# A delta-rule attention, mixture and decay attention kernel: the delta loop's instruction queues rearranged, decay tables stored inside the loop, and the decay attention's key scaling moved to GpSimd

## The chip, the core and the metric

The kernel runs on 1 core of one Trainium2 chip. The metric is the device time of one execution in microseconds (us); the median of several executions is given. All data is fp32.

## The reference

The input `x` has 4 batches of 1024 tokens with 128 channels. Four blocks are added to it, each of the layer-normed `x`:

```
x = x + delta_attention(layernorm(x))     # 8 heads of 128, 3 key/value pairs per token
x = x + mixture(layernorm(x))             # 15 experts of 128, softmax router, best 3, one shared expert
x = x + decay_attention(layernorm(x))     # 2 heads of 64
x = x + mixture(layernorm(x))
```

The delta attention, for each head, token by token (q, k and v come from a projection, a causal convolution of 4 taps and a silu; k and q are normed; `gt` is a decay, `bt` a step size):

```
S = S * exp(gt)
for i in range(3):
    S = S + bt_i * outer(k_i, v_i - k_i @ S)
o = q @ S;  out = (rmsnorm(o) * rms_weight * silu(gate)) @ Wo
```

The decay attention, for each head, token by token: `state = (1 - w)[:, None] * state + outer(k, v); out = r @ state`, where `w` and `r` are sigmoids of projections.

## The kernel before

The program has five stages, each a block of five instruction queues (TensorE `pe`, ScalarE `act`, VectorE `dve`, GpSimd `pool`, and `sp`, which issues DMAs) that wait for each other through semaphores. Each queue runs strictly in the order in which it is written.

**Prologue** (`prologue`). It norms `x` into `g.xn`, and makes the decays. For each of the 8 heads TensorE multiplies (line 213), ScalarE takes the exponential into `g.ex` (line 255) and VectorE masks the result (line 355, 128x1024 elements). The masked table of a head is stored to memory as four DMAs of 128 KB (`keep_table`, line 129): three from SP, one from ScalarE. The loop reads these tables back (`dec_load`, lines 541 and 542), each head's when its first step comes.

**Delta attention** (`delta_attention`). The work of a head is cut into 16 steps of 64 tokens of all 4 batches (two chunks of 32 tokens each, `cc` 0 and 1), so there are 128 steps. A software pipeline runs over `f`. In one frame every engine does one piece of three steps: the newest step `f` (keys and query: `k_tile`, `tap0` to `tap3`, `ktr`, `ksum_`, `es_`, `kr`, `gram`, `ap`), a step `c = f - 11` (values and the inverse of a triangular matrix: `v_tile`, `vtr`, `vr`, `zm`, `zev`, `wm`, `w12`, `m3`, `yev`), and the step `r = c - 1` before it, which goes through the recurrence. The recurrence of one step is, for `cc` 0 and then 1: `ks` (TensorE, line 1068), `rhs_` (VectorE, 901), `w_` (TensorE, 1078), `wev` (ScalarE, 762, writes `ws`), `sr` (TensorE, 1088), and `sup` (VectorE, 912, writes the new state `S`, with `Sg` from GpSimd's `sg`, 675). The outputs `o_` (TensorE, 1103 and 1104) go through `mo_` (ScalarE, 820), `fo_` (GpSimd, 684 and 686), `osb_` (828), `ot` (1221), `og_` (1001), `out` (1228) and `acc_` (1009).

GpSimd's `subst` (707 and 710) does the substitution inside triangular blocks of 32 rows for groups of four steps; once per group, so in every fourth frame, ScalarE copies a finished group transposed (`xt`, line 862, 96x1024) and SP stores it.

`m3` (line 1213) is eight small matrix products of 96 rows, with 64 columns of `Zt` as weights and 32 moving columns, and of its result only 32 rows are used (`yev` and the copies before it). The order of a frame is a list of calls per engine at the end of each block, written by hand or by a search; nothing else sets it.

**Mixture** (`normed_mixture`), twice, which the change does not touch.

**Decay attention** (`decay_attention`). Eight tiles of 512 tokens are projected (`tile`), into the tiles `rF`, `kB`, `F` and `V`. Then, for each batch, levels 0 to 7 double the length of the blocks whose tokens may see each other. A level below `MASKED` = 7 is a near step: TensorE multiplies 64-wide squares (`near`, line 1757), VectorE merges them under a mask into `Pc` (1945 for level 0, `COPY_PREDICATED` at 1948 for the others), and VectorE then scales `kB`, `rF` and `F` for the next level (`merge`, lines 1962, 1963 and 1965, 128x512 elements each). Level 7 is a far step: TensorE multiplies just the new corner (1770), ScalarE copies it straight into `P` (1861), VectorE only scales. `spread` (1869, ScalarE) copies `Pc` into `P` once a batch's last near step is done. Levels 0 and 1 of batches 0 to 2 are put between the tiles, everything else behind them. At the end TensorE turns `kB` (1791) and the outputs are made.

## Time and profile before

| | us |
|---|---|
| median of 3 runs (3137.80 to 3139.36) | 3138.93 |
| the profiled execution, its own time | 3139.86 |
| its span in the trace | 3138.0 |
| TensorE busy (93% of the span) | 2919.0 |
| VectorE busy (79%) | 2486.9 |
| ScalarE busy (75%) | 2346.9 |
| GpSimd busy (63%) | 1977.9 |

The profiled execution is one of its own, 0.9 us slower than the median. Its span begins with the first instruction on the core. The prologue takes it from 0 to 72.5 us, the delta loop to 2417, the first mixture to 2680, the decay attention to about 2860 and the second mixture to the end. "Busy" is the time in which an engine has at least one instruction running, so a queue that has no gap in the trace can still be slowed by the gaps that its own pipeline leaves.

### The profile page before, as it was taken

How to read it: one execution, taken by the hardware profiler on the slowest of the kernel's cores; microseconds unless marked ns; L12 is line 12 of the kernel's file. 1: busy time of each engine (PE TensorE's matmuls, PEld its weight loads, DVE VectorE, ACT ScalarE, POOL GpSimd, SP SyncE). 2: the span in 40 equal slices, each digit the busy share in tenths (PEclk: the TensorE clock that was granted, in tenths of full speed). 3: DMA queues.
4: the chain of work that ended last, by engine and by line, in shares of the span. 5: the costliest groups of instructions: out<-in, count | busy, mean ns of one | idle time of the engine just before them, and what ended most of it. 6: DMA issues, size and time to landing. Idle time of an engine off the chain costs nothing. (4 is left out here: it accounts for less than half of the span.)

```text
span 3138.0 us, 84065 instructions
## 1 busy us (share of the span) xinstructions
PE 2919.0 (93%) x27212; PEld 2241.5 (71%) x27212; DVE 2486.9 (79%) x5731; ACT 2346.9 (75%) x7723; POOL 1977.9 (63%) x3127
## 2 busy tenths in 40 slices
PE   5569999999999999999999999999987999768999
PEld 3448888888888888888888888888776444455444
DVE  5669999999999999999999999999754455594544
ACT  4769999999999999999999999999754443314443
POOL 1588888888888888888888888888831000100000
PEclk8779999999999999999999999999998999868999
DMA  5457777777777777777777777777532323002242
GB/s 108 123 147 179 190 187 180 180 184 174 184 187 191 182 182 182 178 179 182 193 184 182 183 179 182 180 189 181 154 96 75 152 102 152 10 3 78 107 160 115
DMA packets 588208, 482.91 MB, mean 154 GB/s; under 512 B 464784, under 2 KB 504368, under 8 KB 581632
## 3 DMA queue, kind: packets, MB, share of 16 engines
q1 hardware_dynamic: 579328, 474.39, 57.4%
q8 instruction: 223, 3.65, 0.5%
q10 hardware_dynamic: 8448, 3.15, 0.4%
q14 instruction: 209, 1.71, 0.2%
HBM read 285.53 MB, written 191.86 MB: 152 GB/s over the span
## 5 line engine op out<-in xcount | busy, mean ns | idle before, releaser
L953 DVE SCALAR_TENSOR_TENSOR conv_k<-PP,tk,conv_k 128x256 f32<-128x256 f32 x1536 | 718.5, 479 | 101.0 <-ACT conv_k L772 75.7
L953 DVE SCALAR_TENSOR_TENSOR conv_v<-PP,tv,conv_v 128x256 f32<-128x256 f32 x1152 | 540.5, 478 | 57.4 <-ACT conv_v L772 43.1
L710 POOL TENSOR_TENSOR X<-X,tmp 96x31 f32<-96x31 f32 (+15 forms) x992 | 534.3, 539 | 77.8
L707 POOL TENSOR_TENSOR tmp<-At,X 96x31 f32<-96x31 f32 (+15 forms) x992 | 486.7, 491 | 63.3 <-DMA At<-n_d 5.1
L1114 PE MATMUL PP<-xn,wk 128*128 128x268 f32 x1024 | 342.5, 418 | 41.4 <-DVE conv_k L953 29.7
L675 POOL TENSOR_TENSOR Sg<-S,gend 128x512 f32<-128x512 f32 x256 | 266.6, 1041 | 63.3 <-DVE S L912 63.3
L744 ACT ACTIVATE recA<-TG,es 96x128 f32<-96x128 f32 x1024 | 285.0, 367 | 6.3 <-DVE es L946 6.3
L693 POOL TENSOR_TENSOR rk<-ss,half 96x8 f32<-96x8 f32 x128 | 209.0, 1633 | 125.9 <-DVE ss L921 119.6
L1078 PE MATMUL RB<-rhs,Yf 96*96 96x128 f32 x2048 | 269.7, 274 | 18.7 <-DVE rhs L901 18.4
L772 ACT ACTIVATE conv_k<-PP,tk 128x256 f32<-128x256 f32 x512 | 245.2, 480 | 46.6 <-PE PP L1114 26.1
L1068 PE MATMUL RA<-S,kqgB 128*96 128x128 f32 x2048 | 276.1, 278 | 1.0 <-DVE S L912 1.0
L736 ACT ACTIVATE recA<-TG 128x128 f32<-128x128 f32 x1024 | 267.0, 309 | 9.8 <-PE TG L1165 9.6
L1088 PE MATMUL RA<-ws,recB 96*128 96x128 f32 x2048 | 273.8, 277 | 0.2 <-ACT ws L762 0.2
L1078 PEld LDWEIGHTS RB<-rhs,Yf 96*96 96x96 f32 x2048 | 241.9, 163 | 42.9 <-DVE rhs L901 30.3
L1088 PEld LDWEIGHTS RA<-ws,recB 96*128 96x128 f32 x2048 | 262.2, 194 | 8.0 <-ACT ws L762 0.6
L1177 PE MATMUL TG<-kq 128*96 128x128 f32 x1888 | 254.2, 277 | 1.7 <-ACT recA L744 1.5
L736 ACT ACTIVATION_READ_ACCUMULATOR recA<-TG 128x1 f32 x1024 | 245.8, 243 | 0.0
L1068 PEld LDWEIGHTS RA<-S,kqgB 128*96 128x96 f32 x2048 | 233.6, 163 | 12.9 <-DVE S L912 4.1
L1177 PEld LDWEIGHTS TG<-kq 128*96 128x96 f32 x1888 | 215.6, 163 | 19.7 <-ACT recA L744 7.9
L660 POOL TENSOR_TENSOR kqgA<-kq,gdec 128x768 f32<-128x768 f32 x128 | 203.5, 1590 | 34.0 <-ACT kq L813 26.0
L1114 PE MATMUL PP<-xn,wv 128*128 128x268 f32 x768 | 220.1, 394 | 1.2 <-DVE conv_k L953 1.2
L1114 PEld LDWEIGHTS PP<-xn,wk 128*128 128x128 f32 x1024 | 162.5, 198 | 72.3 <-issue 32.0
(292 smaller groups left out, 6578.4 us busy)
## 6 DMA issues: line engine op xcount, KB each, us to landing
kqg_d<-kqgA SPq DMA_DIRECT2D x128, 512.0 KB, 6.4
kqgB<-kqg_d SPq DMA_DIRECT2D x128, 512.0 KB, 4.4
rec_d<-recA SPq DMA_DIRECT2D x128, 480.0 KB, 3.4
recB<-rec_d SPq DMA_DIRECT2D x128, 480.0 KB, 6.1
f1gates<-f1gates_d SPq DMA_DIRECT2D x24, 1024.0 KB, 6.8
f2gates<-f2gates_d SPq DMA_DIRECT2D x24, 1024.0 KB, 6.9
gdec<-gdec_d SPq DMA_DIRECT2D x128, 128.0 KB, 5.8
apk_d<-apkA SPq DMA_DIRECT2D x128, 128.0 KB, 3.3
```

Source lines behind the costliest of these rows:

```text
L675: nc.gpsimd.tensor_tensor(Sg[:, :, :], S[cc][:, :, :], d.broadcast_to([128, B, 128]), ALU.mult).then_inc(sg_ev[cc], 1)
L707: nc.gpsimd.tensor_tensor(t, At[q % 2][:, j, j + 1:].unsqueeze(2).broadcast_to(sh), X[q % 2][:, j, 0:cols].unsqueeze(1).broadcast_to(sh), ...
L710: nc.gpsimd.tensor_tensor(x, x, t, ALU.subtract).then_inc(sub_ev, 1)
L736: last = nc.scalar.activation(recA[N % 2][:, u * 128:(u + 1) * 128], TG[:, u, :], ACT.Square, accum_out=ksum[:, u:u + 1])
L744: last = nc.scalar.activation(recA[N % 2][0:R, u * 128:(u + 1) * 128], TG[0:R, u, :], ACT.Copy, scale=es[:, u, TC - 1:TC])
L772: nc.scalar.activation(acc, src[:, :, 0:SPAN], ACT.Copy, scale=w).then_inc(tap0_ev[i], 1)
L953: return nc.vector.scalar_tensor_tensor(acc, src[:, :, j:j + SPAN], w[:, j:j + 1], acc, ALU.mult, ALU.add)
L1068: last = mm(RA[0:R, b, :], kqgB[N % 2][:, b * NCC + cc, 0:R], S[cc][:, b, :], start=True, stop=True)
L1078: last = mm(RB[0:R, b, :], Yf[N % 2][:, b * NCC + cc, :], rhs[:, b, :], start=True, stop=True)
L1088: last = mm(RA[:, b, :], recB[N % 2][:, u * 128:(u + 1) * 128], ws[cc][:, b, :], start=True, stop=True)
L1114: mm(out, w, x, start=True, stop=True).then_inc(tile_mm[i], 1)
L1177: last = mm(gram_bank(N, hf)[0:R, u % HU, :], kq[N % 2][:, u, 0:R], kq[N % 2][:, u, :], start=True, stop=True)
```

## The change

1. The decay tables. Before the loop only head 0's table is stored; the tables of heads 1 to 7 are stored by SP from inside the loop, four DMAs at the head of each of the frames 1 to 7. The masking of heads 1, 3, 5 and 7 moves from VectorE to GpSimd.
2. The delta loop. Every engine's list is a new one. The frame is cut at another point, so that the lists name `f - 1` where they named `f` before, and one more turn of the loop is made. `mo_` of both halves stands behind `o_` of both halves, `o_` of half 1 no longer waits for `mo_` of half 0 (`osq` has one slot per half for that), and `m3` takes 32 columns of weights in place of 64.
3. The decay attention. `MASKED` is 6, so level 6 (the last merge of blocks of 32 rows) becomes a far step; the scaling of `kB` moves from VectorE to GpSimd (`keys`), and VectorE's scaling of `F` waits for it; 11 near steps in place of 6 stand between the tiles.

```diff
@@ prologue
-            for h in range(NH):
-                sp.wait_ge(mask_ev, h + 1)
-                for b in range(B - 1):
-                    keep_table(sp, h, b)
+            sp.wait_ge(mask_ev, 1)
+            for b in range(B - 1):
+                g.keep_table(sp, 0, b)
...
+            for h in range(1, NH, 2):
+                pool.wait_ge(ex_ev, h + 1)
+                x = ex[:, h, :].rearrange("p (c t) -> p c t", t=TC)
+                nc.gpsimd.tensor_tensor(x, x, upto, ALU.mult).then_inc(odd_ev, 1)
...
@@ delta_attention
-        osq = sb("osq", [128, 128])
+        osq = sb("osq", [128, NCC, 128])
...
+            def tables(h):
+                if 0 < h < NH:
+                    for b in range(B):
+                        keep_table(sp, h, b)
...
-            for f in range(NF):
+            for f in range(NF + 1):
                 r, c = f - BACK - 1, f - BACK
-                at_load(*group_at(f, GROUP + 1))
-                x_store(*group_at(f, 2 * GROUP + 1))
-                rec_load(c)
+                weights(*divmod(f, KSTEPS))
+                tables(f)
+                rec_load(c - 1)
+                dec_load(f - 1)
+                at_load(*group_at(f - 1, GROUP + 1))
+                y_load(c)
+                ap_store(f - 2)
+                kqg_store(f - 2)
+                rec_store(f - 2)
+                x_store(*group_at(f - 1, 2 * GROUP + 1))
                 da_load(c + 1)
-                weights(*divmod(f, KSTEPS))
-                dec_load(f)
-                kqg_store(f - 1)
-                rec_store(f - 1)
-                ap_store(f - 1)
-                y_load(c + 1)
...
-                x_zero(*group_at(f, 3))
                 fo_(r - 1)
-                kqg(f - 1)
+                rk_(f - 2)
+                kqg(f - 2)
                 sg(r, 0)
-                rk_(f - 1)
-                subst(*group_at(f, GROUP + 1), range(0, 6))
+                subst(*group_at(f - 1, GROUP + 1), range(0, 6))
                 sg(r, 1)
-                subst(*group_at(f, GROUP + 1), range(6, 12))
+                x_zero(*group_at(f - 1, 3))
+                subst(*group_at(f - 1, GROUP + 1), range(6, 12))
...
-                need(act, o_mm[cc], N)
+                need(act, o_mm[1], N)
...
-                if cc:
-                    need(pe, mo_ev[0], N)
-                else:
+                if not cc:
                     need(pe, acc_ev, N - 1)
...
-                    last = mm(spot(u, 32, 64), Zt[:, u, :], Yf[N % 2][:, u, 64:96], start=True, stop=True)
+                    last = mm(ZW[64 * (u // HU):64 * (u // HU) + 32, u % HU, 32:64], Zt[:, u, 0:32], Yf[N % 2][:, u, 64:96], start=True, stop=True)
...
@@ decay_attention
-    MASKED, W = 7, 64
+    MASKED, W = 6, 64
...
+        WITHIN = [[], [], [(0, 0)], [(1, 0), (2, 0)], [(0, 1), (3, 0)], [(1, 1), (4, 0)], [(0, 2), (2, 1)], [(1, 2), (3, 1)]]
...
+            def keys(l, b):
+                if not l:
+                    return
+                pool.wait_ge(up_ev, ups[l - 1, b] + 1)
+                pool.wait_ge(p_mm, products(l, b) + 1)
+                k = halves(kB, l, b)[:, :, 0, :]
+                nc.gpsimd.tensor_tensor(k, k, last_of_half(l, b, 1), ALU.mult).then_inc(kup_ev, 1)
...
-                nc.vector.tensor_tensor(kv[:, :, 0, :], kv[:, :, 0, :], end, ALU.mult)
-                nc.vector.tensor_tensor(rv[:, :, 1, :], rv[:, :, 1, :], mid, ALU.mult).then_inc(t_ev, 1)
...
+                nc.vector.tensor_tensor(r, r, mid, ALU.mult)
+                dve.wait_ge(kup_ev, kups[l, b] + 1)
+                nc.vector.tensor_tensor(f, f, mid, ALU.mult).then_inc(up_ev, 1)
```

The lists of TensorE, ScalarE and VectorE are shown by what they make of a frame. A row is one instruction or a run of equal ones: its line, its operation, the tiles out<-in and the shape. On **TensorE**, from `vtr` (`TG<-ident,vt`) to the gate's projection (`PP<-xn,wg`). Before:

```order
L1187 MATMUL TG<-ident,vt 96x128 x8
L1088 MATMUL RA<-ws,recB 96x128 x4
L1114 MATMUL PP<-xn,wv 128x268 x2
L1165 MATMUL TG<-ident,kq 128x128 x4
L1068 MATMUL RA<-S,kqgB 96x128 x4
L1165 MATMUL TG<-ident,kq 128x128 x4
L1196 MATMUL ZW<-Dd,apkB 64x64 x8
L1221 MATMUL SD<-ident,osb 128x128 x2
L1078 MATMUL RB<-rhs,Yf 96x128 x4
L1114 MATMUL PP<-xn,wv 128x268
L1228 MATMUL SD<-og,wo 128x256
L1114 MATMUL PP<-xn,wg 128x256
```

After:

```order
L1100 MATMUL RA<-ws,recB 128x128 x4
L1197 MATMUL TG<-ident,vt 96x128 x4
L1124 MATMUL PP<-xn,wv 128x268 x2
L1206 MATMUL ZW<-Dd,apkB 64x64 x8
L1197 MATMUL TG<-ident,vt 96x128 x4
L1175 MATMUL TG<-ident,kq 128x128 x4
L1080 MATMUL RA<-S,kqgB 96x128 x4
L1175 MATMUL TG<-ident,kq 128x128 x4
L1124 MATMUL PP<-xn,wv 128x268
L1231 MATMUL SD<-ident,osb 128x128 x2
L1090 MATMUL RB<-rhs,Yf 96x128 x4
L1124 MATMUL PP<-xn,wg 128x256
```

`sr` of half 1 (`RA<-ws,recB`) is now ahead of `vtr`, `vtr` is cut in two, and `zm` (`ZW<-Dd,apkB`) stands between its halves, ahead of `ks` (`RA<-S,kqgB`); the third `v_tile` comes before `w_` (`RB<-rhs,Yf`). The `o_` products, which stood apart (half 0 between two `k_tile`s, half 1 before `m3`), now stand together with `m3` between them.

On **ScalarE**, from `ksilu` (`kq<-conv_k`, three keys) to `gate_` in a frame with the transposed copy `At<-X`. Before:

```order
L804 ACTIVATE kq<-conv_k 128x3x8x32
L813 ACTIVATE kq<-conv_k 128x8x32
L862 ACTIVATE At<-X 96x1024
L772 ACTIVATE conv_v<-PP,tv 128x256 x2
L828 ACTIVATE osb<-SD,fo 128x128 x2
L736 ACTIVATE recA,ksum<-TG 128x128 x8
L762 ACTIVATE ws<-RB 96x512
L772 ACTIVATE conv_v<-PP,tv 128x256
L794 ACTIVATE gate<-PP 128x4x2x32
```

After:

```order
L816 ACTIVATE kq<-conv_k 128x3x8x32
L784 ACTIVATE conv_v<-PP,tv 128x256 x2
L825 ACTIVATE kq<-conv_k 128x8x32
L874 ACTIVATE At<-X 96x1024
L840 ACTIVATE osb<-SD,fo 128x128 x2
L748 ACTIVATE recA,ksum<-TG 128x128 x8
L784 ACTIVATE conv_v<-PP,tv 128x256
L774 ACTIVATE ws<-RB 96x512
L806 ACTIVATE gate<-PP 128x4x2x32
```

The copy moved behind the first two value taps (`conv_v<-PP,tv`), and `ws` of half 0 behind the third.

On **GpSimd** in the decay attention, from the fourth tile on. Before, a root and a `MEMSET` for each tile were all:

```order
L1898 TENSOR_TENSOR b_rs<-b_var,b_mhalf 128x4
L1899 MEMSET b_P 128x1024
L1898 TENSOR_TENSOR b_rs<-b_var,b_mhalf 128x4
L1899 MEMSET b_P 128x1024
L1898 TENSOR_TENSOR b_rs<-b_var,b_mhalf 128x4
```

After:

```order
L1921 TENSOR_TENSOR b_rs<-b_var,b_mhalf 128x4
L1922 MEMSET b_P 128x1024
L1930 TENSOR_TENSOR b_kB<-b_kB,b_F 128x512
L1930 TENSOR_TENSOR b_kB<-b_kB,b_F 128x256x2
L1921 TENSOR_TENSOR b_rs<-b_var,b_mhalf 128x4
L1922 MEMSET b_P 128x1024
L1930 TENSOR_TENSOR b_kB<-b_kB,b_F 128x128x4
L1921 TENSOR_TENSOR b_rs<-b_var,b_mhalf 128x4
```

The scaling of the keys (28 in all) now stands in GpSimd's queue, between the roots that each next tile's norm waits for.

## Rows read from the trace of the kernel before

**Rows 1.** Stretch, its length, busy us of PE, PEld, DVE, ACT, POOL, clock, DMA

```profile
300.00:1000.00 700.00, 691.54 (x7296) 582.66 (x7298) 647.15 (x1505) 645.06 (x2238) 610.20 (x974) 1.00 0.73 183
```

**Rows 2.** Timeline, TensorE, one ordinary frame: start us, us, engine, line, tiles

```profile
1019.34 1.08 PE L1187 MATMUL TG<-ident,vt 128*96 128x128 f32 x8
...
1025.66 0.62 PE L1114 MATMUL PP<-xn,wv 128*128 128x268 f32 x2
1026.12 0.59 PE L1228 MATMUL SD<-og,wo 128*128 128x256 f32 x2
...
1027.88 0.62 PE L1114 MATMUL PP<-xn,wk 128*128 128x268 f32 x2
1028.43 0.45 PE L1103 MATMUL SD<-S,kqgB 128*32 128x128 f32 x8
...
1036.28 1.08 PE L1187 MATMUL TG<-ident,vt 128*96 128x128 f32 x8
```

**Rows 3.** Timeline, the frame before it, with the transposed copy

```profile
1001.05 1.08 PE L1187 MATMUL TG<-ident,vt 128*96 128x128 f32 x8
...
1003.29 2.02 ACT L862 ACTIVATE At<-X 96x1024 f32<-96x1024 f32 x1
...
1005.83 1.00 DVE L953 SCALAR_TENSOR_TENSOR conv_v<-PP,tv,conv_v 128x256 f32<-128x256 f32 x2 [1.38 <-ACT conv_v L772]
```

**Rows 4.** Timeline, weight loads of o_ half 1 and of m3

```profile
1018.29 0.26 PEld L1104 LDWEIGHTS SD<-ws,recB 96*32 96x32 f32 x8
...
1018.75 0.55 PEld L1213 LDWEIGHTS ZW<-Yf,Zt 96*64 96x64 f32 x16 [0.20 <-issue]
```

**Rows 5.** Timeline near 201 us, VectorE and GpSimd

```profile
201.41 1.58 POOL L660 TENSOR_TENSOR kqgA<-kq,gdec 128x768 f32<-128x768 f32 x1
201.50 2.19 DVE L921 TENSOR_SCALAR ss<-ksum 128x8 f32<-128x8 f32 x1 [3.71 <-ACT recA L736]
202.94 0.71 POOL L661 TENSOR_TENSOR kqgA<-kq,gdec 128x256 f32<-128x256 f32 x1
```

**Rows 6.** Timeline, end of the prologue

```profile
49.76 21.45 SPq L129 DMA_DIRECT2D edec_d<-ex  x24
...
63.08 1.22 DVE L355 TENSOR_TENSOR ex<-ex,p_upto 128x1024 f32<-128x1024 f32 x1 [0.86 <-ACT ex L255]
72.53 0.55 SPq L541 DMA_DIRECT2D edec<-edec_d  x1
```

**Rows 7.** Groups of the whole program: busy us, mean ns of one, idle before

```profile
L675 POOL TENSOR_TENSOR Sg<-S,gend 128x512 f32<-128x512 f32 x256 | 266.6, 1041 | 63.3 <-DVE S L912 63.3
```

**Rows 8.** Timeline, one near step of the decay attention

```profile
2768.99 1.34 DVE L1948 COPY_PREDICATED b_Pc<-b_masks,b_pair 128x1024 f32<-128x1024 uint32 x1
...
2769.22 1.99 PE L1757 MATMUL b_pair<-b_rF,b_kB 64*64 64x64 f32 x64 [1.66 <-DVE b_F L1965]
2770.21 0.69 DVE L1962 TENSOR_TENSOR b_kB<-b_kB,b_F 128x512 f32<-128x512 f32 x1
2770.81 0.69 DVE L1963 TENSOR_TENSOR b_rF<-b_rF,b_F 128x512 f32<-128x512 f32 x1
...
2772.15 1.33 DVE L1948 COPY_PREDICATED b_Pc<-b_masks,b_pair 128x1024 f32<-128x1024 uint32 x1
```

**Rows 9.** Timeline, ScalarE's spread and far copies at the end of the levels

```profile
2823.86 2.13 ACT L1869 ACTIVATE b_P<-b_Pc 64x1024 f32<-64x1024 f32 x2 [1.01 <-DVE b_Pc L1948]
2826.02 3.75 ACT L1861 ACTIVATE b_P<-b_pair 64x1024 f32<-64x1024 f32 x4
```

**Rows 10.** Timeline, TensorE, a frame of the loop's tail, where no new keys come

```profile
2283.22 0.59 PE L1228 MATMUL SD<-og,wo 128*128 128x256 f32 x2
...
2288.92 1.11 PE L1078 MATMUL RB<-rhs,Yf 96*96 96x128 f32 x8 [0.78 <-DVE rhs L901]
...
2292.82 1.06 PE L1088 MATMUL RA<-ws,recB 96*128 96x128 f32 x8
...
2298.16 0.59 PE L1228 MATMUL SD<-og,wo 128*128 128x256 f32 x2
```

More of the change, by code:

```diff
@@ L1228, in out @@
                 mm(SD[:, 0:256], wo[N // KSTEPS % 2][:, :], og[:, :], start=True, stop=True).then_inc(out_mm, 1)
-            for f in range(NF):
+            for f in range(NF + 1):
                 r, c = f - BACK - 1, f - BACK
+                ks(r - 1, 1)
+                gram(f - 2, 0)
+                w_(r - 1, 1)
+                k_tile(f - 1, 2)
+                k_tile(f - 1, 3)
+                o_(r - 1, 0)
+                m3(c - 1)
+                o_(r - 1, 1)
+                gram(f - 2, 1)
+                sr(r - 1, 1)
+                vtr(c - 1, 0)
                 v_tile(c, 0)
                 v_tile(c, 1)
+                zm(c)
+                vtr(c - 1, 1)
+                ktr(f - 1, 0)
+                ks(r, 0)
                 ktr(f - 1, 1)
-                ks(r, 0)
-                ktr(f - 1, 0)
-                zm(c)
+                v_tile(c, 2)
                 ot(r - 1)
                 w_(r, 0)
-                v_tile(c, 2)
+                gate_tile(c)
                 out(r - 1)
-                gate_tile(c)
                 sr(r, 0)
                 k_tile(f, 1)
-                o_(r, 0)
                 k_tile(f, 0)
                 wm(c)
-                ks(r, 1)
-                gram(f - 1, 0)
-                k_tile(f, 2)
-                w_(r, 1)
-                gram(f - 1, 1)
-                k_tile(f, 3)
-                o_(r, 1)
-                m3(c)
-                vtr(c, 1)
-                vtr(c, 0)
-                sr(r, 1)
 def normed_mixture(nc, g, tag, last=False):
@@ L1658, in decay_attention @@
         NP = NEAR + len(FAR)
-        pair_of = lambda n: 3 if n < 2 * B else n % 4
+        WITHIN = [[], [], [(0, 0)], [(1, 0), (2, 0)], [(0, 1), (3, 0)], [(1, 1), (4, 0)], [(0, 2), (2, 1)], [(1, 2), (3, 1)]]
+        TIGHT = sum(len(w) for w in WITHIN)
+        pair_of = lambda n: 3 if n < TIGHT else n % 4
         before = {n: max((m for m in range(n) if pair_of(m) == pair_of(n)), default=None) for n in range(NP)}
@@ L1675, in steps @@
                 yield "tile", i
-                for l in range(2):
-                    b, odd = divmod(i - 2 - l, 2)
-                    if not odd and 0 <= b < B - 1:
-                        yield "near", (l, b)
-            yield "near", (0, B - 1)
-            yield "near", (1, B - 1)
-            for l in range(2, LV + 1):
+                for x in WITHIN[i]:
+                    yield "near", x
+            done = [x for w in WITHIN for x in w]
+            for l in range(LV + 1):
                 for b in range(B):
-                    yield ("near" if l < MASKED else "far"), (l, b)
+                    if (l, b) not in done:
+                        yield ("near" if l < MASKED else "far"), (l, b)
         order = [x for kind, x in steps() if kind == "near"]
         near_no = {x: n for n, x in enumerate(order)}
-        ups = {}
+        ups, kups = {}, {}
         for kind, x in steps():
@@ L1691, in decay_attention, with halves, last_of_half, products @@
                 ups[x] = len(ups)
+                if x[0]:
+                    kups[x] = len(kups)
+        def halves(t, l, b):
+            return t[:, b * T:(b + 1) * T].rearrange("p (n two h) -> p n two h", two=2, h=1 << (l - 1))
+        def last_of_half(l, b, right):
+            hs = 1 << (l - 1)
+            return halves(F, l, b)[:, :, right, hs - 1:hs].broadcast_to([128, T // (2 * hs), hs])
+        def products(l, b):
+            return near_no[l, b] if l < MASKED else far_no[l, b]
         @block.tensor
@@ L1857, in far @@
                 act.wait_ge(p_mm, n + 1)
+                act.wait_ge(spread_ev, 128 // W * (b + 1))
                 for c in range(0, 128, 2 * H):
@@ L1880, in _ @@
                 spread(b)
-            for b in range(B):
-                far(LV, b)
+            for l, b in FAR:
+                far(l, b)
             for q in range(NG // 4):
@@ L1892, in _, with root @@
         def _(pool):
-            nc.gpsimd.memset(mhalf[:, :], -0.5).then_inc(mhalf_ev, 1)
-            pool.wait_ge(mhalf_ev, 1)
-            for i in range(NT):
+            def root(i):
+                if i >= NT:
+                    return
                 pool.wait_ge(ve_ev, i + 1)
@@ L1899, in _ @@
                 nc.gpsimd.memset(P[:, 4 * i:4 * i + 4, :, :], 0.0).then_inc(cleared, 1)
+            def keys(l, b):
+                if not l:
+                    return
+                pool.wait_ge(up_ev, ups[l - 1, b] + 1)
+                pool.wait_ge(p_mm, products(l, b) + 1)
+                k = halves(kB, l, b)[:, :, 0, :]
+                nc.gpsimd.tensor_tensor(k, k, last_of_half(l, b, 1), ALU.mult).then_inc(kup_ev, 1)
+            nc.gpsimd.memset(mhalf[:, :], -0.5).then_inc(mhalf_ev, 1)
+            pool.wait_ge(mhalf_ev, 1)
+            root(0)
+            for kind, x in steps():
+                if kind == "tile":
+                    root(x + 1)
+                else:
+                    keys(*x)
         @block.vector
```

128 lines of the change are left out of this document (62 added, 66 removed).

## Prediction

> **What bounds the kernel now.** I read the busy times first: TensorE is busy for 93% of the span, the others for 63 to 79%. These are means over five stages, so I read the stretches next. In the delta loop from 300 to 1000 us [rows 1] TensorE is busy for 691.5 of 700 us at the full clock of 2.4 GHz; VectorE has 647, ScalarE 645 and GpSimd 610. The loop is bound by what TensorE issues, but three engines have only 8 to 13% left, so a new order can turn any of them into the bound.
>
> Then the timeline of single frames. From `vtr` to `vtr` an ordinary frame takes 1036.28 - 1019.34 = 16.94 us [rows 2]; the one before it, with the transposed copy, 1019.34 - 1001.05 = 18.29 [rows 3]. Every fourth frame is of the second kind, so the mean is (3 x 16.94 + 18.29)/4 = 17.28 us. All three pieces run in frames 11 to 127; I count 116 full ones. One microsecond in the mean frame is thus 116 us of the kernel, and 0.054 us are 0.2% of it, which is about what a measurement of this kernel can tell from no change.
>
> **The order of the loop, ordinary frames.** The matrix products are the same in number and columns, only `m3` has narrower weights. Two things could shorten the frame.
>
> First, switches between small and large products. `k_tile` starts at 1027.88 and the `o_` behind it at 1028.43: 0.55 us [rows 2], where the two products back to back elsewhere take 0.46 (`v_tile` at 1025.66, `out` at 1026.12). So small groups that stand alone cost about 0.09 each, and the new order brings the two `o_` groups and `m3` together. It also cuts `vtr` in two, which gives some back. I take -0.05, between -0.15 and +0.1.
>
> Second, `m3`. Sixteen of its weight loads take 0.55 us, 0.034 each; the eight loads of `o_` half 1, which are just as narrow as the new ones, 0.26, 0.033 each [rows 4]. By these a narrower load saves nothing; by the width alone it would be half of 0.55 = 0.27. I take -0.05, since the loads lie beside products of the same tiles and the rows show that they hardly depend on the width.
>
> Together -0.1: 16.84.
>
> **Frames with the copy.** The copy of `X` takes ScalarE 2.02 us [rows 3]. Behind it, the value tap on ScalarE comes late, and VectorE waits 1.38 us for it; that is also nearly the 1.35 us by which the frame is longer. In the new order the first two value taps are ahead of the copy, but `osb`, `ksum`, the third value tap and `ws` of half 0 are still behind it, and `ws` feeds `sr`, which TensorE now issues earlier. ScalarE's own work in such a frame, 645/700 of 17.28 = 15.9 on average and 15.9 + 0.75 x 2.02 = 17.4 with the copy [rows 1, 3], leaves no room for a return to 16.84. I take 18.05, between 17.4 and 18.6.
>
> The mean becomes (3 x 16.84 + 18.05)/4 = 17.14, or 0.14 less. 116 x 0.14 = **-17 us**. The bounds are -45 (mean 16.89) and +45 (mean 17.67, the slower rival).
>
> What could take it back are small operations on VectorE. The one on `ss` took 2.19 us for 8 elements in a partition: it started at 201.50 and ended at 203.69, with GpSimd's two scalings over at 202.99 and 203.65 [rows 5]. The new order puts such an operation beside GpSimd's work again, as the old one does, so I price no change. The Trainium skill ("SBUF — State Buffer", section on the two separate sides) says that GpSimd and a VectorE instruction that needs the shared port pair lock each other out for a whole instruction; by that rule the trace agrees in these rows. GpSimd's and SP's lists are also new, but GpSimd is busy for 87% and SP mostly waits; each store or load there has a frame or more until it is needed. Cost 0; if that cover fails it is the slower rival's kind.
>
> **Prologue.** The last of the 24 table stores on SP ends at 49.76 + 21.45 = 71.21 and the loop's first load stands at 72.53, while the last mask on VectorE ends at 63.08 + 1.22 = 64.30 [rows 6]. Without the stores of heads 1 to 7 the loop's start hangs on the masks, or on SP's own work ahead of it. Half of the masks go to GpSimd, where I estimate 2 x 1.04 = 2.1 us for 1024 elements from the 1041 ns of `Sg` with 512 [rows 7]; that is slower than VectorE's 1.22, but the two work side by side and each waits for ScalarE's exponentials. I put the start between 64.5 and 72.5 and take 67.5: **-5 us** (-8 to 0). The 28 stores come back in frames 1 to 7, four per frame: 4 x 21.45/24 = 3.6 us of SP [rows 6], in frames where only keys run and SP mostly waits. Cost 0; with that cover gone, up to 3 us a frame for 7 frames, 20 us, at the far end of the range.
>
> The early frames get the same small gain and the tables' load; 0, between -8 and +8. The extra turn of the loop holds no work of its own.
>
> **The loop's tail.** The last twelve frames have no new keys; one takes 2298.16 - 2283.22 = 14.94 us [rows 10]. TensorE waits there 0.78 us for `rhs`, so it is the recurrence that sets the frame. In the old order `sr` of half 1, at 2292.82, comes after `vtr`, whose eight products take 1.08 us [rows 2]; in the new one `vtr` is behind it, so it comes 1.1 us sooner, or somewhat more. But `ks` then has both halves of `vtr`, two `v_tile`s and `zm` ahead of it, which gives back part of it. I take -0.7 a frame, between nothing and twice that, **-8 us** in all (-17 to 0).
>
> **Decay attention.** In the near steps VectorE is the bound: TensorE waits 1.66 us for `F`, and a step takes 2772.15 - 2768.99 = 3.16 us [rows 8]. It is the merge 2770.21 - 2768.99 = 1.22, the keys 2770.81 - 2770.21 = 0.60, and 1.34 for `rF` and `F`. The change takes the keys from VectorE 28 times, 28 x 0.60 = 16.8, and the merges of level 6 four times, 4 x 1.22 = 4.9: 21.7 us. On GpSimd the same scaling should cost 1.04 us [rows 7], which fits beside the 1.22 of the next merge. Given back: ScalarE has to copy the corners of four more far steps, and such a copy of four takes 3.75 us against 2.13 for two spreads [rows 9]; most lies beside VectorE's work of other batches, only the last batch's stands in the chain, about 5. And `F` has to wait for GpSimd's semaphore 28 times; with a lag of about 0.15 each, 4 more. That makes **-13 us** (-22 to 0). The five near steps more between the tiles cost VectorE the same there as behind: 0.
>
> The mixtures are as they were.
>
> **Sum.** -17 - 5 - 8 - 13 = -43 against the profiled execution's 3139.9 is 3096.9. That execution was 0.9 above the median, so **3096.0 us**.
>
> **The rivals.**
>
> *The loop gains more* (0.22). If the lone small groups and the narrow weights are worth what the high bounds say, the ordinary frame is 16.6 and the one with the copy 17.7: mean 16.88, 116 x 0.40 = -46 in place of -17, 3067 us. For it: 8.5 us in 700 without any product and 0.09 at each switch [rows 1, 2]. Against it: the work itself is the same.
>
> *The loop gains nothing* (0.15). The old frame already has TensorE busy throughout, so an order may do nothing: mean 17.28, and only the rest is left, -26: 3113 us. For it: 98.8% busy [rows 1], and narrow loads as long as wide ones [rows 4].
>
> *The keys cost on GpSimd what they save on VectorE* (0.08). If VectorE stands still while GpSimd scales, as in the `ss` row [rows 5], each scaling costs its full 1.04 in place of 0.60: 28 x 1.04 = 29.1 against 21.7 saved, so the decay attention gets 7 us slower, 20 worse than in my sum: 3116. The skill's rule of the locked port pair, above, asks for this, as both engines would read two tiles of SBUF. Against it: the merge's source is `pair`, which TensorE writes, so it may not need what GpSimd holds. The Trainium skill ("GPSIMD Engine Reference", section 4.1) also sends elementwise work to VectorE, as GpSimd needs about twice the time for two inputs; here, 1.04 to 0.60, the trace agrees.
>
> *Slower: `sr` waits for `ws` in every frame* (0.09). In the new list `ws` of half 0 stands behind eight `ksum` copies and the third value tap on ScalarE, and `sr` of the same half comes soon after `w_` on TensorE. ScalarE is busy for 92%, and its key work hangs on VectorE operations that GpSimd can hold for 2 us [rows 5]. If TensorE waits 0.4 us a frame more than now, the mean is 17.68: 116 x 0.40 = +46, with -26 from the rest +20: 3159 us. It decides from a mean frame of 17.28 + 26/116 = 17.50 on. Against it: I find some slack, 0.05 to 0.2 us, at each of these places when I lay the durations out, but not much.
>
> **How the numbers follow.** My forecast has 0.46, the rivals 0.22, 0.15, 0.08 and 0.09. The range takes in my forecast with its bounds, the larger gain and the two small gains, and leaves the far end of the larger one and the slower rival out: 3062 to 3130. Faster by over 0.2% (below 3132.6) is 0.86: all but the slower rival and a mishap of tables and order together. Within 0.2% 0.05, slower by over 0.2% (above 3145.2) 0.09.
>
> **What would show it.** The loop's first load on SP at about 67.5 us. `vtr` to `vtr` 16.84 us in an ordinary frame, 18.05 with the copy. VectorE's wait for the value tap behind the copy is gone; a new one of TensorE's `sr` for `ws` should be there in frames with the copy only, below 1 us. `m3`'s loads still at 0.03 us each. Tail frames at 14.2 us. Near steps at 2.55 us, with GpSimd's keys at about 1.04 and `F` waiting at most 0.2. I am wrong if the mean frame is over 17.28, if frames 1 to 7 grow by more than 1 us each, or if the keys on GpSimd take much over 1.2 us or hold `rF`'s scaling on VectorE.

## The result and the profile after

| | before | changed |
|---|---|---|
| median, us | 3139.14 (4 runs, 3137.80 to 3143.02) | 3061.40 (4 runs, 3060.88 to 3067.43) |
| ratio, 95% interval | | 0.9755 (0.9738 to 0.9772) |
| the profiled execution, its own time | 3139.86 | 3067.43 |
| its span | 3138.0 | 3065.5 |
| TensorE / VectorE / ScalarE / GpSimd busy | 2919.0 / 2486.9 / 2346.9 / 1977.9 | 2853.1 / 2420.3 / 2355.9 / 2034.5 |

The changed kernel is 2.45% faster, 78 us by the medians. Its profiled execution was the longest of the four, by 6 us. The forecast was 43 us. Stage by stage, from the same starts in both traces (first `k_tile`, first and last `og`, the first `MEMSET` of each stage behind the loop):

| stage | before | changed | difference | forecast |
|---|---|---|---|---|
| prologue, to TensorE's first product of the loop | 72.6 | 70.2 | -2.4 | -5 |
| from there to the first `og` | 176.5 | 182.3 | +5.8 | 0 |
| first `og` to the 116th | 1982.8 | 1940.4 | -42.4 | -17 |
| 116th to the last (128th) | 184.9 | 165.4 | -19.5 | -8 |
| decay attention | 192.7 | 177.8 | -14.9 | -13 |

These make -73.4; the mixtures and the joins give +0.9, which is the -72.5 of the spans. The loop gave more than twice its share.

Not all of the last row is the change's. The decay attention of the kernel before, which by the marks of this table ends at 2872.7 and not at about 2860, took 192.7 us in this trace, with a granted clock of 0.76. In the six `b_` kernels below, whose decay attention is the same, it took 188.7 to 190.3 us at 0.77 to 0.78; in the changed kernel the clock there was 0.83. So up to 4 of the 14.9 us lie between executions of the same code.

Stretch of the delta loop in the changed kernel, columns as in [rows 1]:

```profile
300.00:1000.00 700.00, 689.86 (x7453) 581.35 (x7452) 639.28 (x1537) 662.95 (x2299) 626.19 (x995) 1.00 0.71 187
```

In the same 700 us at the same full clock there are 7453 products in place of 7296, and TensorE's busy share is no higher. Busy time alone would not have told that the frame could shrink.

Timeline of TensorE around a frame with the copy and the next one, with one wait of VectorE (start us, us, line, tiles), the rows that answer to [rows 2] and [rows 3]:

```profile
1002.68 0.45 PE L1113 MATMUL SD<-S,kqgB 128*32 128x128 f32 x8
...
1013.16 0.48 DVE L965 SCALAR_TENSOR_TENSOR conv_v<-PP,tv,conv_v 128x256 f32<-128x256 f32 x1 [1.14 <-ACT conv_v L784]
1013.67 1.16 PE L1100 MATMUL RA<-ws,recB 96*128 96x128 f32 x8 [0.55 <-ACT ws L774]
...
1015.67 0.69 PE L1215 MATMUL ZW<-Yf,Zt 96*64 96x64 f32 x16
...
1020.15 0.45 PE L1113 MATMUL SD<-S,kqgB 128*32 128x128 f32 x8
1020.40 0.42 PE L1114 MATMUL SD<-ws,recB 96*32 96x128 f32 x8
1020.62 0.44 PE L1223 MATMUL ZW<-Yf,Zt 96*32 96x32 f32 x16
1020.87 0.44 PE L1113 MATMUL SD<-S,kqgB 128*32 128x128 f32 x8
1021.09 0.44 PE L1114 MATMUL SD<-ws,recB 96*32 96x128 f32 x8
1021.46 1.11 PE L1187 MATMUL TG<-kq 128*96 128x128 f32 x8
...
1032.31 0.69 PE L1215 MATMUL ZW<-Yf,Zt 96*64 96x64 f32 x16
```

An ordinary frame, from `wm` to `wm`, takes 1032.31 - 1015.67 = 16.64 us; the frame with the copy, from `o_` to `o_`, 1020.15 - 1002.68 = 17.47. The mean over 112 frames is 16.87, before it was 17.25. The wait of `sr` for `ws` that the slower rival spoke of is there, but only in the frame with the copy (0.55 us here, 0.54 to 0.70 over such frames); in an ordinary frame its weight loads wait 0.22 us and its products not at all. VectorE's wait behind the copy is not gone: it has moved from the first value tap (1.38 us [rows 3]) to the third (1.14 us). From the first `o_` to the next large product, both `o_` and `m3` take 1021.46 - 1020.15 = 1.31 us.

TensorE's weight loads in the same place:

```profile
1020.29 0.26 PEld L1114 LDWEIGHTS SD<-ws,recB 96*32 96x32 f32 x8
1020.51 0.43 PEld L1223 LDWEIGHTS ZW<-Yf,Zt 96*32 96x32 f32 x16
1020.84 0.20 PEld L1113 LDWEIGHTS SD<-S,kqgB 128*32 128x32 f32 x8
1021.46 0.90 PEld L1187 LDWEIGHTS TG<-kq 128*96 128x96 f32 x8 [0.20 <-issue]
```

The first three follow each other without a gap. In [rows 4], where `m3`'s 64-wide loads came after the 32-wide ones of `o_`, the last `o_` load ended at 1018.55 and `m3`'s began at 1018.75. The same 0.20 us now stands once a frame, behind the second `o_`, where 96-wide loads follow.

### The profile page after: what moved, and what is told of

It reads as the page before. It is cut to its first block and busy times, and to the rows that moved or that the text cites. A ratio compares the mean times of both kernels' runs of the same rounds, so it can differ in the third digit from the quotient of the medians.

```text
span 3065.5 us, 84106 instructions
## 1 busy us (share of the span) xinstructions
PE 2853.1 (93%) x27212; PEld 2185.9 (71%) x27212; DVE 2420.3 (79%) x5695; ACT 2355.9 (77%) x7731; POOL 2034.5 (66%) x3159
## 5 line engine op out<-in xcount | busy, mean ns | idle before, releaser
L965 DVE SCALAR_TENSOR_TENSOR conv_k<-PP,tk,conv_k 128x256 f32<-128x256 f32 x1536 | 671.1, 478 | 123.8 <-ACT conv_k L784 109.6
L965 DVE SCALAR_TENSOR_TENSOR conv_v<-PP,tv,conv_v 128x256 f32<-128x256 f32 x1152 | 523.0, 471 | 58.5 <-ACT conv_v L784 51.6
L1124 PE MATMUL PP<-xn,wk 128*128 128x268 f32 x1024 | 295.6, 411 | 49.8 <-DVE conv_k L965 43.4
L1100 PE MATMUL RA<-ws,recB 96*128 96x128 f32 x2048 | 283.4, 281 | 18.9 <-ACT ws L774 18.9
L756 ACT ACTIVATE recA<-TG,es 96x128 f32<-96x128 f32 x1024 | 273.8, 370 | 21.7 <-DVE es L958 21.6
L1100 PEld LDWEIGHTS RA<-ws,recB 96*128 96x128 f32 x2048 | 249.1, 192 | 54.7 <-ACT ws L774 52.4
L1187 PE MATMUL TG<-kq 128*96 128x128 f32 x1888 | 263.9, 283 | 0.5 <-ACT recA L756 0.5
L784 ACT ACTIVATE conv_k<-PP,tk 128x256 f32<-128x256 f32 x512 | 227.8, 474 | 28.7 <-PE PP L1124 14.8
L1090 PEld LDWEIGHTS RB<-rhs,Yf 96*96 96x96 f32 x2048 | 233.9, 163 | 12.4 <-DVE rhs L913 12.1
L748 ACT ACTIVATION_READ_ACCUMULATOR recA<-TG 128x1 f32 x1024 | 219.4, 214 | 0.0
```

What stands on the lines that cost most here:

```text
L748: last = nc.scalar.activation(recA[N % 2][:, u * 128:(u + 1) * 128], TG[:, u, :], ACT.Square, accum_out=ksum[:, u:u + 1])
L756: last = nc.scalar.activation(recA[N % 2][0:R, u * 128:(u + 1) * 128], TG[0:R, u, :], ACT.Copy, scale=es[:, u, TC - 1:TC])
L784: nc.scalar.activation(acc, src[:, :, 0:SPAN], ACT.Copy, scale=w).then_inc(tap0_ev[i], 1)
L965: return nc.vector.scalar_tensor_tensor(acc, src[:, :, j:j + SPAN], w[:, j:j + 1], acc, ALU.mult, ALU.add)
L1090: last = mm(RB[0:R, b, :], Yf[N % 2][:, b * NCC + cc, :], rhs[:, b, :], start=True, stop=True)
L1100: last = mm(RA[:, b, :], recB[N % 2][:, u * 128:(u + 1) * 128], ws[cc][:, b, :], start=True, stop=True)
```

## The experiments

"a_" kernels are the changed kernel with one edit, "b_" kernels the one before. Where a kernel has one execution only, its frames are compared and not its total.

### m3's width, in the new order and in the old

In the new order:

```diff
-                    last = mm(ZW[64 * (u // HU):64 * (u // HU) + 32, u % HU, 32:64], Zt[:, u, 0:32], Yf[N % 2][:, u, 64:96], start=True, stop=True)
+                    last = mm(spot(u, 32, 64), Zt[:, u, :], Yf[N % 2][:, u, 64:96], start=True, stop=True)
```

> The changed kernel with m3 back at 64 columns of weights, its place between the two o_ groups kept. Theory W (the narrow weights let two column groups of the array work side by side, and that is where most of the loop's gain came from): the sixteen products take about 0.59 us again in place of 0.25, the ordinary frame goes from 16.65 to about 16.95, the kernel from 3061 to about 3099. Theory P (the place beside o_ gives it, the width nothing, as the prediction took it): the frame stays within 0.05 of 16.65, the kernel within 6 us of 3061.

Measured: 3093.99 us, ratio to before 0.9857 (0.9841 to 0.9872). Ordinary frames 16.79 to 16.85, copy frames 17.83, mean 17.08.

```profile
1010.48 0.45 PE L1113 MATMUL SD<-S,kqgB 128*32 128x128 f32 x8
1010.72 0.42 PE L1114 MATMUL SD<-ws,recB 96*32 96x128 f32 x8
1011.07 0.66 PE L1223 MATMUL ZW<-Yf,Zt 96*64 96x32 f32 x16
1011.66 0.45 PE L1113 MATMUL SD<-S,kqgB 128*32 128x128 f32 x8
1011.90 0.42 PE L1114 MATMUL SD<-ws,recB 96*32 96x128 f32 x8
1012.26 1.11 PE L1187 MATMUL TG<-kq 128*96 128x128 f32 x8
```

The same piece now takes 1012.26 - 1010.48 = 1.78 us, 0.47 more. Its weight loads show where:

```profile
1010.61 0.26 PEld L1114 LDWEIGHTS SD<-ws,recB 96*32 96x32 f32 x8
1011.07 0.55 PEld L1223 LDWEIGHTS ZW<-Yf,Zt 96*64 96x64 f32 x16 [0.20 <-issue]
1011.66 0.18 PEld L1113 LDWEIGHTS SD<-S,kqgB 128*32 128x32 f32 x8
```

The loads stop 0.20 us between `o_`'s 32-wide ones and `m3`'s 64-wide ones, and the sixteen take 0.55 in place of 0.43. The remaining 0.15 lies at the other end: the next `o_` loads begin 0.04 us after `m3`'s (1011.66 against 1011.62), where with the narrow `m3` they begin 0.10 before these end (1020.84 against 1020.94). Of the 0.47 us the ordinary frame feels 0.15 (16.65 to 16.80) and the copy frame 0.35; the rest fills gaps that TensorE has elsewhere (in the changed kernel the weight loads of the second `ktr` stop for 0.27 us in each frame, here they do not). In all the narrow `m3` is worth about 33 us in the new order by the medians, of which the traces place 24 in the full frames and 3 in the tail. So the price of theory W stands, for this order. Its mechanism is not shown: with both widths the outputs of neighbouring products lie at partitions 0 and 64 of `ZW`, and with the wide `m3`, too, the products start in pairs, 7 ns apart. What differs in the rows is the loads.

In the old order, the same edit the other way round:

> The kernel before, m3 alone cut to 32 columns of weights, its place kept. Theory W: ordinary frame 16.90 to about 16.60, copy frame 18.32 to between 18.0 and 18.3, the kernel 3139 to about 3101 to 3110. Theory P: nothing, within 6 us of 3139. If it gives a part only, the width needs the new place to count.

Measured: 3131.97 us (ratio 0.9966, 0.9953 to 0.9979), about 10 us less, and none of it in the full frames: 16.72 to 16.98 and 18.31 to 18.34, the mean 17.239 against 17.251. What it gained lies in the loop's tail (177.3 us against 184.9, a frame there 14.60 against 14.94). The two traces differ by 4 us more in the decay attention, which this edit does not touch. Yet TensorE's piece did get shorter:

```profile
1017.42 0.45 PE L1103 MATMUL SD<-S,kqgB 128*32 128x128 f32 x8
1017.66 0.42 PE L1104 MATMUL SD<-ws,recB 96*32 96x128 f32 x8
1017.89 0.44 PE L1213 MATMUL ZW<-Yf,Zt 96*32 96x32 f32 x16
1018.26 1.08 PE L1187 MATMUL TG<-ident,vt 128*96 128x128 f32 x8
...
1021.06 0.42 PEld L1165 LDWEIGHTS TG<-ident,kq 128*128 128x128 f32 x4 [0.35 <-ACT kq L804]
```

0.84 us in place of 1019.34 - 1018.15 = 1.19. So 0.35 us of TensorE's time came free in each frame and the frame did not follow. The last row shows where it went: `ktr`'s weight loads now wait 0.35 us for ScalarE's silu of the keys, a wait that the kernel before does not have. The old order was held by something beside TensorE. This falls against both theories as they were written.

### What held the old order

A ring is here a path of waits that leads from an operation over other engines back to the same operation of the next frame; the frame cannot be shorter than it. Three kernels take work from one engine each, on top of the narrow `m3` (the first also without it). What they leave out stands in their expectations.

```diff
@@ tap_of (VectorE), b_dve_light and b_narrow_dve_light
+                n = 4 if j == 3 and name in ("k2", "q") else SPAN
@@ vsilu (ScalarE), b_narrow_act_light
+                n = U if N < 1 else U // 2
@@ kqg (GpSimd), b_narrow_pool_light
+                n = U if N < 2 else U // 2
```

> The kernel before, the last tap of k2 and of the query on VectorE done on 4 of 64 tokens of a step (the rest of these two taps is left out), so VectorE has about 0.7 us less in each frame; every wait stays. Theory T (TensorE bounds the ordinary frame before, as the prediction says): 16.86 to 16.94 stays. Theory R (a ring of VectorE, ScalarE and TensorE bounds it, all three nearly full): it stays as well or falls by up to 0.1, since TensorE has no gap to give.

Measured: ordinary frames 16.86 to 16.95, copy frames 18.32, as before. With the wide `m3` VectorE is not the bound of the old kernel's full frames.

> The kernel before with the narrow m3 and the same two taps on 4 of 64 tokens. The narrow m3 alone left the ordinary frame at 16.85 to 16.95. Theory V (VectorE's queue had become the bound): it falls to about 16.6. Theory A (ScalarE's queue is the bound): it stays at 16.9. The frame with the copy should fall in neither case by more than in b_m3_narrow.

Measured: the three ordinary frames of a group are now 16.63, 16.95 and 16.85, the copy frame 18.33. One of three fell, so with the narrow `m3` VectorE stands in that frame's path.

> The kernel before with the narrow m3 and the silu of the values on half of their units (the rest left out), 0.6 us less on ScalarE in each frame. Theory A: the ordinary frame falls from 16.9 to about 16.6 and the one with the copy by 0.3 to 0.6. Theory V: the ordinary frame stays at 16.9. If both light kernels fall, the two engines stand in one ring of waits.

Measured: 16.58, 16.90, 16.85 and 18.01. Again the same one of three fell, and `ktr`'s wait for `kq` is gone from all frames. The two others are those in which ScalarE waits for GpSimd's `fo`:

```profile
1015.90 0.63 ACT L829 ACTIVATE osb<-SD,fo 128x128 f32<-128x128 f32 x2 [1.17 <-POOL fo L686]
1022.05 0.47 ACT L772 ACTIVATE conv_k<-PP,tk 128x256 f32<-128x256 f32 x1 [0.27 <-PE PP L1115]
1032.66 0.63 ACT L829 ACTIVATE osb<-SD,fo 128x128 f32<-128x128 f32 x2 [0.96 <-POOL fo L686]
```

> The kernel before with the narrow m3 and GpSimd's first scaling of kq on half of the units (the rest left out), about 0.8 us less on GpSimd in each frame. Theory G (in the old order GpSimd's queue, without a wait in three frames of four, delivers fo late to ScalarE's osb, and this holds the ordinary frames at 16.85 to 16.95 once TensorE needs less): they fall to about 16.6, the frame with the copy stays near 18.3 or falls little. Rival (ScalarE or TensorE's waits for it hold them): two of the three stay at 16.9, as with the lighter VectorE and the lighter ScalarE.

Measured: 16.85, 16.84, 16.85, 18.32. The 16.95 is gone, but the frames stop at 16.85, with `ktr`'s wait for `kq` as long as before (0.34 us). GpSimd's root `rk` now waits for `ss`, whose inputs wait for `osb` on ScalarE, which waits for `fo`:

```profile
1022.19 1.63 POOL L694 TENSOR_TENSOR rk<-ss,half 96x8 f32<-96x8 f32 x1 [0.33 <-DVE ss L922]
1034.46 0.20 POOL L685 TENSOR_TENSOR fo<-mo,q 128x2 f32<-128x2 f32 x1
1034.74 0.70 POOL L687 TENSOR_TENSOR fo<-fo,minus_half 128x2 f32<-128x2 f32 x1
1039.04 1.63 POOL L694 TENSOR_TENSOR rk<-ss,half 96x8 f32<-96x8 f32 x1 [0.91 <-DVE ss L922]
```

The last experiment cuts that ring:

```diff
-                rk_(f - 1)
                 subst(*group_at(f, GROUP + 1), range(0, 6))
                 sg(r, 1)
+                rk_(f - 1)
```

> The kernel of b_narrow_pool_light (narrow m3, half of GpSimd's key scaling left out) with one more edit: GpSimd's root rk moved from ahead of the first half of the substitution to behind sg of half 1. Theory Q (with GpSimd made lighter, the frame is held by a ring that TensorE is no part of: ss on VectorE, rk and the substitution and fo on GpSimd, osb and ksum on ScalarE, ss again, 1022.19 to 1039.04 = 16.85 us in that trace, with a wait at each passage): ordinary frames fall from 16.85 to about 16.6, TensorE's own time with the narrow m3. Rival (ScalarE's unbroken queue from ws to the silu of the query, which TensorE's turning of kq waits for): they stay at 16.85.

Measured: 16.83, 16.84, 16.86, 18.31 in most groups, and some groups near the head changes longer (the mean 17.29). Theory Q falls as the cause on its own: two of three frames no longer wait for `fo`, and still take 16.85. In such a frame ScalarE runs from `ws` to `ws`, 1057.93 - 1041.10 = 16.83 us, like this:

```profile
1041.10 0.59 ACT L763 ACTIVATE ws<-RB 96x512 f32<-96x512 f32 x1 [0.39 <-PE RB L1079]
1042.57 0.38 ACT L795 ACTIVATE gate<-PP 128x256 f32<-128x256 f32 x1 [0.52 <-PE PP L1115]
1045.21 0.47 ACT L773 ACTIVATE conv_k<-PP,tk 128x256 f32<-128x256 f32 x1 [0.16 <-PE PP L1115]
...
1053.59 0.38 ACT L814 ACTIVATE kq<-conv_k 128x256 f32<-128x256 f32 x1
1054.10 0.63 PE L1166 MATMUL TG<-ident,kq 128*128 128x128 f32 x4
...
1056.86 1.04 PE L1079 MATMUL RB<-rhs,Yf 96*96 96x128 f32 x8
1057.93 0.59 ACT L763 ACTIVATE ws<-RB 96x512 f32<-96x512 f32 x1 [0.53 <-PE RB L1079]
```

ScalarE's queue from `ws` of half 0 to the silu of the query is 1053.97 - 1041.10 = 12.87 us; `ktr` starts 0.13 us behind it; from `ktr` to the end of `w_` TensorE takes the other 3.8 us, and `ws` starts again. ScalarE waits in its part for products of TensorE (0.52 and 0.16 us), but only until 1045.21; from there to `ws` it has no wait. TensorE's `m3` stands beside that stretch, so a shorter `m3` only makes TensorE wait elsewhere (for `kq`, 0.32 us in this frame). The silu of the values stands inside it, and taking half of that silu did shorten the one frame that does not wait for `fo`. So the traces point at two rings of nearly the same length, 16.85 us. This is read from the waits and from which frames fell; that cutting both at once would bring all three frames to 16.6 is argued and was not run.

### The copy frame

> The changed kernel with the transposed copy on ScalarE ahead of the first two value taps again, nothing else moved. If the copy's new place is what took 18.32 to 17.49: the fourth frame goes to about 18.2, others stay at 16.65, the kernel + 29 x 0.7 = 20 us, 3082. Rival, the rest of the new order took it: within 0.2 of 17.49, 3061 to 3067.

Measured (3093.89 us, one execution), one line of ScalarE's list moved: from `og` to `og` the copy frames take 18.36 to 18.40, mostly with one of 16.54 behind; on TensorE's products they take 18.26 in place of 17.49 and the ordinary ones are unchanged. The mean is 17.06 in place of 16.87. The place of the copy is worth 0.19 x 116 = 22 us in the full frames; the trace is 26.5 us longer than the changed kernel's, and 4.6 of the rest are in the tail. `sr` does not wait in this trace, but VectorE does again for the first value tap:

```profile
1017.16 1.27 DVE L965 SCALAR_TENSOR_TENSOR conv_v<-PP,tv,conv_v 128x256 f32<-128x256 f32 x3 [1.51 <-ACT conv_v L784]
```

The copy's new place, behind two of the three value taps, trades this wait for 1.14 us at the third tap and 0.55 us of `sr`, and the frame is 0.8 us shorter. The copy frame of the changed kernel is then ScalarE's own: it is busy for 17.14 of the 17.47 us from 1002.68 on, and TensorE for 16.73. The next kernel takes work out of that frame:

```diff
+            CUTS = [0, 8, 14, 20, BLK]
             def xt(q, k):
-                if q is None or k:
+                if q is None:
                     return
-                act.wait_ge(sub_ev, (BLK - 1) * (q + 1))
-                nc.scalar.activation(At[q % 2][:, :, :], X[q % 2][:, :, :].rearrange("p r c -> p c r"), ACT.Copy).then_inc(xt_ev, 1)
+                lo, hi = CUTS[k], CUTS[k + 1]
+                act.wait_ge(sub_ev, (BLK - 1) * q + hi - 1)
+                last = nc.scalar.activation(At[q % 2][:, :, lo:hi], X[q % 2][:, lo:hi, :].rearrange("p r c -> p c r"), ACT.Copy)
+                if k == GROUP - 1:
+                    last.then_inc(xt_ev, 1)
...
-                xt(*group_at(f - 1, 2 * GROUP + 1))
+                xt(*group_at(f - 1, GROUP + 2))
```

> The changed kernel with the transposed copy cut into four parts by finished rows (8, 6, 6 and 12 of 32), one in each frame, in the same place of ScalarE's list. Theory S (the frame with the copy is bound by ScalarE's own work, 15.5 + 2.0 us, so only taking work out of that frame helps): all frames go to 16.65 to 16.75, the mean from 16.87 to 16.67, 116 x 0.2 = 23 us, 3038. Rival (0.5 us more of ScalarE in every frame pushes ws of half 0 behind TensorE's sr in each): the ordinary frames grow to about 16.9 and nothing is gained.

Measured: 3039.55 us, ratio to before 0.9675 (0.9657 to 0.9692), the fastest kernel here. Most frames are 16.62 to 16.76, the longest 16.93, the mean 16.66, with no longer fourth frame. The substitution works from the first row to the last, so the first rows are final while the last are still worked on, and the part of `At` that the copy overwrites is no longer read.

```profile
300.00:1000.00 700.00, 696.29 (x7564) 589.21 (x7563) 646.35 (x1556) 671.76 (x2355) 631.75 (x1009) 1.00 0.72 189
```

Here ScalarE is busy for 96% and TensorE for 99.5%.

### Prologue and tables

> The changed kernel with the prologue's masks all on VectorE and all tables stored before the loop, as before; the loop stores none. Theory E (the stores in frames 1 to 7 delay the early frames): the loop starts 2.4 us later (72.5), but its first outputs (og) come at 249 and not at 252.5, so the kernel is 3 to 4 us faster than the changed one, 3057. Theory N (the stores in the loop cost nothing): 2 to 5 us slower, 3064.

Measured: 3062.97 us (ratio 0.9757, 0.9741 to 0.9773), no difference from the changed kernel that these runs can tell. The loop starts at 71.9 and the first `og` comes at 250.6: 178.7 us for the early part. Theory E has the early part right and the total wrong, since the prologue gives back as much.

> The changed kernel with all eight masks of the prologue on VectorE, the tables still stored inside the loop. Theory L (GpSimd's masks of 2.3 us hold VectorE's products of two tiles for as long, so the help is none): the loop's TensorE starts at about 66 us in place of 70.1, the kernel 4 us faster, if the early frames keep what they are given. Rival: the loop starts at 70 or later.

Measured: 3058.67 us (ratio 0.9734, 0.9719 to 0.9750), by the medians 2.7 us faster than the changed kernel, with intervals that overlap. The trace is plainer: the loop starts at 64.75, where the five other kernels with tables in the loop start it at 68.2 to 70.2, and the first `og` comes at 246.6, 4 us sooner than in the kernel above. The reason is in the changed kernel's prologue, GpSimd's masks and VectorE beside them:

```profile
50.81 6.68 POOL L272 TENSOR_TENSOR ex<-ex,p_upto 128x1024 f32<-128x1024 f32 x2 [27.18 <-ACT ex L251]
52.42 2.87 DVE L356 TENSOR_TENSOR ex<-ex,p_upto 128x1024 f32<-128x1024 f32 x1 [0.42 <-ACT ex L251]
55.22 4.49 DVE L347 TENSOR_TENSOR p_gm<-p_gt,p_upto 128x1024 f32<-128x1024 f32 x2
```

A mask takes VectorE 1.22 us alone [rows 6], 2.87 here; two `p_gm` 4.49, where the two just before, at 49.65, took 2.35 in the same trace; GpSimd needs 6.68 us for two masks. The two engines take turns rather than work side by side. The Trainium skill ("SBUF — State Buffer", the section on the two separate sides) says that the pair of ports that both use is locked for a whole instruction; by that rule the trace agrees.

With the tables in the loop the early part takes 181.8 to 182.3 us in four traces (183.1 and 183.2 in those of the two kernels whose loop is slower), with them in the prologue 178.7 in the one trace there is: the stores cost 3.1 to 3.6 us there. Their leaving the prologue gave 71.9 - 68.2 = 3.7 in the kernels whose masks are shared by two engines, so the two cancel. The rest of the +5.8, 178.7 against 176.5, goes to the new order; it rests on one trace of each, and in the `b_` kernels this part took 173.2 to 177.2.

### The keys of the decay attention

```diff
-                nc.gpsimd.tensor_tensor(k, k, last_of_half(l, b, 1), ALU.mult).then_inc(kup_ev, 1)
...
+                nc.vector.tensor_tensor(k, k, last_of_half(l, b, 1), ALU.mult)
+                nc.vector.tensor_tensor(r, r, mid, ALU.mult).then_inc(kup_ev, 1)
```

> The changed kernel with the keys of the decay attention scaled by VectorE again; level 6 stays a far step and 11 near steps stay between the tiles. If GpSimd's scaling is worth what VectorE no longer does (28 x 0.60 = 16.8) less what the two engines take from each other (in the profile VectorE's scalings of rF and F grew from 692 to 860 ns, 56 x 0.17 = 9.4): +7 us, 3069. If GpSimd's side costs nothing: +17, 3078. If it costs what it saves: within 3 of 3061, and the 15 us came from level 6 and the steps between the tiles.

Measured: 3072.47 us (ratio 0.9788, 0.9769 to 0.9807), 11 us more by the medians; the stage takes 188.0 us in place of 177.8, both at a clock of 0.83. GpSimd's keys are worth 10 of the 16.8 us that they take from VectorE. The rest of the stage's change, level 6 and the steps between the tiles, is worth little: 188.0 against the 188.7 to 190.3 of the old stage. What the keys lose, they lose where VectorE scales at the same time (changed kernel):

```profile
2730.36 0.67 DVE L1998 TENSOR_TENSOR b_rF<-b_rF,b_F 128x512 f32<-128x512 f32 x1
2730.67 1.32 POOL L1930 TENSOR_TENSOR b_kB<-b_kB,b_F 128x512 f32<-128x512 f32 x1 [0.51 <-PE b_pair L1779]
2730.95 1.59 DVE L2000 TENSOR_TENSOR b_F<-b_F 128x512 f32<-128x512 f32 x1
...
2734.84 1.11 POOL L1930 TENSOR_TENSOR b_kB<-b_kB,b_F 128x512 f32<-128x512 f32 x1 [2.84 <-PE b_pair L1779]
2734.89 1.34 DVE L1988 COPY_PREDICATED b_Pc<-b_masks,b_pair 128x1024 f32<-128x1024 uint32 x1
...
2743.64 4.99 POOL L1930 TENSOR_TENSOR b_kB<-b_kB,b_F 128x512 f32<-128x512 f32 x1 [0.46 <-PE b_pair L1792]
```

`F` takes 1.59 us where it takes 0.69 alone [rows 8], and once GpSimd took 4.99 us for one scaling behind an unbroken run of VectorE's. Beside the merge from PSUM both keep their time, 1.11 and 1.34 us. Over the stage the 56 scalings of `rF` and `F` went from 692 to 860 ns: 56 x 0.168 = 9.4 us. 16.8 less 9.4 would leave 7.4; the 10 measured are 3 more, and where these come from is open.

## Why the prediction was right or wrong

**The total.** The direction held. The median of 3061.4 lies 0.6 us below the low end of the range, and 0.9755 x 3138.93 = 3062.1 just on it; the gain was 1.8 times the forecast: the case that came true is the rival "the loop gains more", which had 0.22 and 3067 us, and not the likeliest.

**The premise.** "The loop is bound by what TensorE issues" failed as a statement on the old order. TensorE was busy for 99% and could still be shortened by 0.35 us a frame without effect; it then waits 0.35 us for ScalarE. By the traces two rings through ScalarE, GpSimd and TensorE had the same 16.85 us, which is argued and not cut in one kernel. The warning that "a new order can turn any of them into the bound" should have been asked of the old order too.

**Ordinary frames.** -0.10 forecast, -0.25 measured (16.90 to 16.65). Both terms were too small: the new order with the wide `m3` gave -0.10 where the sum had -0.05, and the narrow `m3` another -0.15 where it had -0.05. That the two were added was wrong as well: in the mean frame the order alone gave -0.17, the narrow `m3` alone -0.01, both together -0.38. I took the price of the width from loads of 0.034 and 0.033 us, but these compare sixteen loads with eight, and sixteen narrow ones take 0.43 us and not 2 x 0.26. The rows I quoted [rows 4] also held the largest single part of the price, the gap of 0.20 us ahead of the wide loads. With the same width throughout, the piece is 0.47 us shorter than with the wide `m3` in the same place. The Trainium skill ("TensorE: Matmul & The Clock Gate", "Why this matters for your kernels") advises to put each small output at 32 partitions of its own, in a column group of its own, so that products run side by side. No run here tests that, as both widths of `m3` have their outputs in two separate groups.

**The copy frame.** -0.24 forecast, -0.81 measured (18.30 to 17.49). I named the mechanism (VectorE's 1.38 us wait behind the copy goes) and then set most of it against `ws`, which held TensorE for 0.55 to 0.70 us only. The wait did not go, it moved to the third tap (1.14 us), where it costs less. 0.46 of the 0.81 came with the new order and the wide `m3`, 0.35 with the narrow one, for which this frame had no term of its own. My floor for ScalarE of 17.4 was right: the frame landed on it, at 17.49, and only cutting the copy up went below.

**The tail.** -0.7 a frame forecast, -0.95 measured (14.94 to 13.99), and the longer frames between them (16.53 and 17.82 before), which I had not looked at, went as well: -19.5 in place of -8. 0.43 of each frame is the narrow `m3` (14.42 without it), which the sum did not have here; the order alone gave -0.52 of its -0.7.

**Prologue and early frames.** The loop's start was forecast at 67.5; it came at 68.2 to 68.8 in four further kernels with this prologue and at 70.2 in the profiled execution of the changed one. "Cost 0" for the tables was wrong by some 3.5 us, and the new order seems to cost the early frames 2 more. That the masks "work side by side" was wrong, at a price of 3 to 4 us.

**Decay attention.** -13 forecast, -14.9 measured in the two profiled executions, -10.9 to -12.5 against the `b_` kernels. The near agreement is in part luck: the keys were worth 10 where the sum had 16.8 less 4 for the handshake, and the loss was another one. VectorE stood idle ahead of `F` for 1.0 us in all, not 4, but its scalings took 9.4 us longer. A scaling of the keys took GpSimd 1.58 us on average, not 1.04, so the sign of being wrong that I had named ("much over 1.2 us") came. The rival by which the port lock eats the whole gain did not come: the lock is seen, but the merge from PSUM is free of it and hides most of GpSimd's time.

**The other rivals.** The slower one's wait exists, 0.54 to 0.70 us in every fourth frame; in the others TensorE's products do not wait for `ws`. The one by which the loop gains nothing rested on TensorE's 98.8%, and the old order, in which TensorE's time could shrink and the frame not, shows that this share proves nothing.

## What to carry to other kernels

An engine that is busy for 99% in a software pipeline may be only one of several rings of the same length. Before a gain on it is priced, follow one frame from a wait on each engine back to itself and see whether the saved time lies inside every ring that has the frame's length; a kernel with the saving alone in the old order tells it in one run, and a new wait in its trace shows where the saved time went. Two edits that each give little can give much together, so price a pair as a pair. Read the gaps of the weight loads as well as their lengths, try small products of one width side by side in the list, and cut a long periodic operation into parts where its inputs become final in order. Give GpSimd work beside operations of VectorE that read PSUM (the merge kept its 1.34 us), not beside those with two SBUF operands (0.69 us became 1.59).
